# Turning the first chunk's residual by VectorE blocks and a trip through memory in place of four TensorE transposes

## The reference, cut to what matters

```
xn = layernorm(layernorm(x)) * ln_g + ln_b
q, k, v = split(xn @ W_qkv + b_qkv)
gate = sigmoid(layernorm(x) @ W_gate + b_gate); gate /= mean(gate) + 1e-5
q, k = relu(q * gate)**2 + 1e-5, relu(k * gate)**2 + 1e-5
# scan over time, per head: kv += k^T v; ks += k; out = (q @ kv) / (q . ks + 1e-5)
x1 = x + out @ W_proj + b_proj
P = layernorm(x1) @ U1                    # 512 -> 128
H = gelu(P @ V1 + b1)                     # 128 -> 2048
out = x1 + (H @ U2) @ V2 + b2             # 2048 -> 128 -> 512
```

## Time and profile before

| | |
|---|---|
| median of the runs | 1697.15 us |
| profiled execution | 1697.67 us, of which the span of the trace is 1695.9 us |
| PE busy | 1665.1 us (98%) |
| DVE busy | 1400.3 us (83%) |
| POOL, ACT busy | 900.2 us (53%), 630.5 us (37%) |
| x1t_lo, line 683 | 64 times, mean 681 ns |
| key blocks, line 737 | 64 times, mean 703 ns |

### The profile page before, as it was taken

One profiled execution on the slowest core, in us unless ns is written; L12 is line 12 of the kernel. 1 busy time (PEld: TensorE's weight loads), 2 busy tenths in 40 slices (PEclk: granted clock), 3 DMA queues, 4 the chain that ended last, 5 costly groups with the idle time before them and its releaser, 6 DMA issues.

```text
span 1695.9 us, 39553 instructions
## 1 busy us (share of the span) xinstructions
PE 1665.1 (98%) x16221; PEld 1401.9 (83%) x16221; DVE 1400.3 (83%) x2223; ACT 630.5 (37%) x1178; POOL 900.2 (53%) x1026
## 2 busy tenths in 40 slices
PE   6899999999999999999999999999999999999998
PEld 4688888888888888888888888888888888888876
DVE  6888888888888888888888888888888888888875
ACT  4233333333333333433433333333333333333332
POOL 3355555555555555555555555555555555555540
PEclk9999999999999999999999999999999999999999
DMA  8323323333322333342333233343223323322210
GB/s 231 88 58 70 59 75 46 72 75 57 72 72 45 74 70 60 73 71 47 74 72 59 73 62 56 74 69 61 74 49 69 75 57 70 74 45 73 58 45 26
DMA packets 206324, 115.67 MB, mean 68 GB/s; under 512 B 151144, under 2 KB 161792, under 8 KB 206144
## 3 DMA queue, kind: packets, MB, share of 16 engines
q1 hardware_dynamic: 205280, 111.57, 31.4%
q10 hardware_dynamic: 864, 1.57, 0.5%
HBM read 79.38 MB, written 33.72 MB: 67 GB/s over the span
## 4 chain that ended last, share of the span: by engine, by line
PE 93%; DVE 3%; DMA 1%; issue 1%; SPq 1%; ACT 0%; POOL 0%; DVEq 0%; POOLq 0%
PE ps_a L849 11%; PE ps_a L850 10%; PE ps_a L851 10%; PE scores L849 8%; PE scores L851 8%; PE scores L850 8%; PE ps_h L849 4%; PE ps_h L850 4%; PE ps_h L851 4%; PE scores L980 4%; PE scores L1008 4%; PE ps_q L849 3%; PE ps_q L850 3%; PE ps_q L851 3%; PE scores L856 3%; PE ps_a L1026 2%
## 5 line engine op out<-in xcount | busy, mean ns | idle before, releaser
L447 POOL TENSOR_TENSOR h_lo<-h_full,h_hi 128x512 fp32r<-128x512 f32 x244 | 336.4, 1389 | 220.4 <-DVE h_hi L665 219.0
L849 PE MATMUL ps_a<-wx_hi,zt_hi 128*128 128x512 f32 x768 | 315.7, 411 | 6.3 <-DVE key_sums L787 4.2
L850 PE MATMUL ps_a<-wx_lo,zt_hi 128*128 128x512 f32 x768 | 305.1, 397 | 0.0
L851 PE MATMUL ps_a<-wx_hi,zt_lo 128*128 128x512 f32 x768 | 305.0, 397 | 0.0
L530 ACT ACTIVATE h_full<-ps_h,cols 128x256 f32<-128x256 f32 x512 | 204.5, 476 | 144.1 <-PE ps_h L851 137.6
L849 PEld LDWEIGHTS ps_a<-wx_hi,zt_hi 128*128 128x128 f32 x768 | 145.3, 189 | 43.2 <-DVE zt_lo L620 7.1
L665 DVE CAST h_hi<-h_full 128x512 fp32r<-128x512 f32 x256 | 163.3, 648 | 17.8 <-ACT h_full L530 13.7
L851 PEld LDWEIGHTS ps_a<-wx_hi,zt_lo 128*128 128x128 f32 x768 | 145.1, 189 | 35.6
L850 PEld LDWEIGHTS ps_a<-wx_lo,zt_hi 128*128 128x128 f32 x768 | 145.3, 189 | 28.7 <-issue 0.5
L541 ACT ACTIVATE query_t<-scores 128x512 f32<-128x512 f32 x64 | 38.3, 599 | 345.9 <-PE scores L856 345.9
L467 POOL TENSOR_TENSOR key_lo<-keys,key_hi 128x512 fp32r<-128x512 f32 x64 | 86.9, 1358 | 121.1 <-ACT key_hi L561 121.1
(11 more groups left out here) (156 smaller groups left out, 4230.7 us busy)
## 6 DMA issues: line engine op xcount, KB each, us to landing
xs<-L_attn_x SPq DMA_DIRECT2D x64, 256.0 KB, 4.1
key_blocks<-zs SPq DMA_DIRECT2D x64, 256.0 KB, 2.0
key_t<-key_blocks SPq DMA_DIRECT2D x256, 64.0 KB
out<-x1s SPq DMA_DIRECT2D x64, 256.0 KB, 2.1
xt<-x_turned SPq DMA_DIRECT2D x63, 256.0 KB, 4.2
key_sums<-carry_rows SPq DMA_DIRECT2D x60, 256.0 KB, 3.7
rows<-turned_rows SPq DMA_DIRECT2D x63, 64.0 KB, 4.5
x1s<-L_attn_W_gate SPq DMA_DIRECT2D x4, 256.0 KB, 4.2
```

The costliest lines, as they stand in the source:

```text
L447: E.tensor_tensor(h_lo[:, i % SLOTS, :], h_full[:, i % SLOTS, :], h_hi[:, i % SLOTS, :].bitcast(F32), ALU.subtract).then_inc(s["h_lo_ready ...
L849: E.matmul(ps, wh, mh, start=start and i == 0, stop=False)
L850: E.matmul(ps, wh, ml, start=False, stop=False)
L851: mm = E.matmul(ps, wl, mh, start=False, stop=stop and i == last)
```

## The change

The first chunk of each pair (`half == 0`) isn't turned by PE any more. In the even step DVE turns `zs` in 32 x 32 blocks into the first quarter of `probs`, right behind the gate (`turn_residual`); SP writes that to a new DRAM tensor `residual_blocks` and reads it back into `zs` by four DMAs of 128-byte pieces. ACT makes `x1t_hi` from `zs` late in the same even step, and DVE makes `x1t_lo` from `zs` at the step's end, between the moments of x1 and the new `zs`. The key blocks go to `gate` instead of `zs`, and the second use of `gate` (line 794) waits until they have been written out. The second chunk of each pair is turned as before.

```diff
+    def pair(self, per=1):
+
+        return per * ((4 * self.p + self.off) // 2 + 1)
...
@@ -338,6 +343,14 @@
+                d = Chunk(p, b - 2)
+                if d.exists and d.half == 0:
+
+                    sp.wait_ge(s["res_out"], d.pair(16))
+                    for j in range(HPG):
+                        sp.dma_start(zs[j * HEAD:(j + 1) * HEAD, :].rearrange("d (f a t) -> d f a t", f=KT, t=HEAD),
+                                     res_dram.rearrange("(a d) (f j t) -> j d f a t", d=HEAD, f=KT, t=HEAD)[j])\
+                            .then_inc(res_in[j], 16)
...
-                    sp.dma_start(blocks_dram, zs[:, :]).then_inc(s["blocks_out"], 16)
+                    sp.dma_start(blocks_dram, gate[:, :]).then_inc(s["blocks_out"], 16)
...
+                before = Chunk(p, b - 1)
+                if before.exists and before.half == 0:
+
+                    sp.wait_ge(s["res_ready"], before.pair())
+                    for j in range(HPG):
+                        wait(sp, res_in[j], before.pair(16) - 16)
+                    sp.dma_start(res_dram, probs[:, 0, :]).then_inc(s["res_out"], 16)
                 load_x(Chunk(p, b + 3))
...
@@ -546,8 +566,8 @@
-                if d.exists:
-                    act.wait_ge(s["tx_done"], d.done())
+                if d.exists and d.half:
+                    act.wait_ge(s["tx_done"], d.pair())
                     E.activation(x1t_hi[:, :, d.half * P:(d.half + 1) * P],
                                  ps_t[:, :].rearrange("p (k n) -> p k n", k=KT), ACT.Copy)\
                         .then_inc(s["x1t_hi_ready"], 1)
...
                     gelu(ffn, pairs[2])
                     gelu(ffn, pairs[3])
+                if d.exists and d.half == 0:
+                    for j in range(HPG):
+                        act.wait_ge(res_in[j], d.pair(16))
+                    E.activation(x1t_hi[:, :, 0:P], zs[:, :].rearrange("p (k n) -> p k n", k=KT), ACT.Copy)\
+                        .then_inc(s["x1t_hi_ready"], 1)
+                if ffn.exists:
...
+                def x1t_from_bank():
+                    if d.half:
+                        x1t_tail(ps_t)
+
+                def turn_residual():
+
+                    if d.exists and d.half == 0:
+                        dve.wait_ge(s["z1_ready"], d.done())
+                        E.transpose(probs[:, 0, :], zs[:, :]).then_inc(s["res_ready"], 1)
...
                         .then_inc(s["gate_evac"], 1)
+                    turn_residual()
 
                     dve.wait_ge(s["gate_sig"], n.done())
...
-                    if d.exists:
-                        dve.wait_ge(s["tx_done"], d.done())
-                    elif c.exists:
-                        dve.wait_ge(s["blocks_out"], c.done(16, 16))
-                    else:
-                        dve.wait_ge(s["tz_done"], 1)
-                    E.transpose(zs[:, :], keys[:, n.half, :]).then_inc(s["blocks_ready"], 1)
+                    E.transpose(gate[:, :], keys[:, n.half, :]).then_inc(s["blocks_ready"], 1)
                 if c.exists:
                     dve.wait_ge(s["scores_done"], c.done())
                     blocks = HPG * KT
+                    if d.exists and d.half == 0:
+                        dve.wait_ge(s["res_out"], d.pair(16))
...
                     dve.wait_ge(s["query_steps"], n.done(3, 3))
+                    dve.wait_ge(s["blocks_out"], n.done(16, 16))
...
                     E.bn_aggr(moments1[:, :], stats1[:, :]).then_inc(s["x1_steps"], 1)
+                if d.half == 0:
+                    x1t_tail(zs)
+                if c.exists:
                     dve.wait_ge(s["x1_small"], c.done(2, 2))
-                    if d.exists:
-                        dve.wait_ge(s["tx_done"], d.done())
+                    if d.exists and d.half == 0:
+                        dve.wait_ge(s["x1t_ready"], d.done())
+                    if d.exists and d.half:
+                        dve.wait_ge(s["tx_done"], d.pair())
                     elif not c.p and not c.off:
                         dve.wait_ge(s["tz_done"], 1)
-                    if n.exists:
-                        dve.wait_ge(s["blocks_out"], n.done(16, 16))
...
```

More of the change, by code:

```diff
@@ L108, in block_kernel @@
 def block_kernel(nc, x, ln_g, ln_b, w_qkv, b_qkv, w_gate, b_gate, w_proj, b_proj,
-                 u1, v1, b1, u2, v2, b2, x_turned, out, carry_dram, rows_dram, blocks_dram):
+                 u1, v1, b1, u2, v2, b2, x_turned, out, carry_dram, rows_dram, blocks_dram, res_dram):
     ctx = ExitStack()
@@ L207, in block_kernel @@
             query_done query_steps value_done value_ready
-            sums_done den_steps blocks_ready blocks_out tq_done query_t_ready
+            sums_done den_steps blocks_ready blocks_out res_ready res_out tq_done query_t_ready
             scores_done probs_ready state_done state_ready ot_done ot_hi_ready ot_ready
@@ L215, in block_kernel @@
         xt_in = [sem(f"xt_in{i}") for i in range(4)]
+        res_in = [sem(f"res_in{j}") for j in range(HPG)]
         key_t_in = [sem(f"key_t_in{j}") for j in range(HPG)]
@@ L677, in step, with x1t_tail @@
                 finishing = is_last(p)
-                def x1t_tail():
+                def x1t_tail(turned):
                     if d.exists:
@@ L682, in x1t_tail @@
                         part = slice(d.half * P, (d.half + 1) * P)
-                        E.tensor_tensor(x1t_lo[:, :, part], ps_t[:, :].rearrange("p (k n) -> p k n", k=KT),
+                        E.tensor_tensor(x1t_lo[:, :, part], turned[:, :].rearrange("p (k n) -> p k n", k=KT),
                                         x1t_hi[:, :, part].bitcast(F32), ALU.subtract).then_inc(s["x1t_ready"], 1)
+                def x1t_from_bank():
[5 more added lines that the diff above has]
+                        E.transpose(probs[:, 0, :], zs[:, :]).then_inc(s["res_ready"], 1)
                 if n.exists:
@@ L704, in step @@
                     squared_relu(n, s["key_done"], s["key_steps"], ps_b, KEY, keys[:, n.half, :],
-                                 x1t_tail)
+                                 x1t_from_bank)
                 else:
-                    x1t_tail()
+                    turn_residual()
+                    x1t_from_bank()
                 if b % 2:
@@ L1070 @@
     blocks_dram = nc.dram_tensor("key_blocks", (P, DM), _mybir.dt.float32, kind="Internal").ap()
+    res_dram = nc.dram_tensor("residual_blocks", (P, DM), _mybir.dt.float32, kind="Internal").ap()
     rows_dram = nc.dram_tensor("turned_rows", (BATCHES, P), _mybir.dt.float32, kind="Internal").ap()
-    block_kernel(nc, *args, out, carry_dram, rows_dram, blocks_dram)
+    block_kernel(nc, *args, out, carry_dram, rows_dram, blocks_dram, res_dram)
     r = _run(nc, [arrays], core_ids=[0])
```

## The result

The changed kernel takes 1688.12 us (median of four runs, 1685.22 to 1688.72) against 1697.08 for the kernel before: ratio 0.9945 (95% interval 0.9928 to 0.9962), 9.0 us gained. Five more rounds on another chip gave 1687.6 against 1695.92, ratio 0.9959 (0.9946 to 0.9972). I had predicted 1682.3 with a range of 1680.3 to 1687. The direction was right, the size wrong by 5.8 us.

The account below looks back on a forecast made before the run. PE was taken to bound the kernel, busy 98% of the span. Gains of 13.2 (steady part), 0.1 (start) and 1.6 (drain) sum to 14.9 us, giving 1682.3 us, range 1680.3 to 1687.

Parts of the forecast that it names:

- What PE loses: PE's stream, each pair: the first chunk's four transposes go, 0.44 us a pair, 13.2 us for 30 pairs.
- The block transpose on DVE: Even step, behind the gate: 0.70 us more on DVE fits into its 1.69 us idle wait for ACT's sigmoid; costs nothing.
- The mask's new wait: DVE's mask in the even step: the residual's write lands in 2.0 us, leaving 4.7 us of slack.
- SP's queue: SP in the even step: x loads start 1.5 us later harmlessly; four reads issued by 838.3, slack 2.1 us.
- the landing of the reads: Reload of `zs` for ACT: lands about 4.8 us after the first issue, over 7 us of slack.
- rival 3: Mask's wait on `res_out`: the trip through memory lands late, at 842.0; 35 us lost against 15 gained, about 1717; 5%.
- The low part in the moments' gap: Even step's end: `x1t_lo` beside POOL's two operations delays the new `zs` by 0.3 us, hidden in the steady part.
- Start: First even step: `x1t_lo` leaves DVE's chain (0.38 us), the gap grows 0.3; gain 0.1, bounds +0.4 and -1.0.
- Drain: Last even step: mask waits for the residual's write, gain 1.9 us, less 0.3 for the gap; net 1.6, bounds 1.9 and 0.
- Rivals 1 and 2: 1: moments' gap too small, 1691.9, 10%. 2: DVE is the real bound, only the drain's gain stays, 1695.6, 5%.

Follow-up runs that it names:

- the drain's edit: Changed kernel with chunk 0's key blocks in `zs`; in the last even step the residual's blocks also go to `gate`, so the mask waits for no write: 1681.84 us.
- the spare products: 8 unused products while PE idles before the mask's first use in the last even step, added to chunk 0's write on ACT's queue and residual in `gate`: 1677.18 us.
- the kernel with three spare writes: Changed kernel with chunk 0's key blocks in `zs`; three extra writes of the turned residual, each landed before the real one is issued: 1841.31 us in one run.

## Why the prediction was wrong, step by step

- *What PE loses*: right. 13.2 predicted for 30 pairs, 14.2 measured (0.47 a pair for 0.44; the 1 us is more than the 0.02 a pair that I allowed for the reading). Other traces with the same steady part have 50.90 a pair, 13.0 in 30.
- *The block transpose on DVE*: right; 0.70 us, and the wait for the sigmoid fell from 1.69 to 1.05 (1.0 predicted).
- *The mask's new wait, SP's queue, the landing of the reads*: right in the steady part. The write's landing had a median of 2.7 us and not 2.0, at most 4.5, all inside the slack. The bound of 4.8 for the reads was misread, as 20 slices of 0.45 us from 1634 end at 1643.0 and not 1643.5; they landed in 2.3 to 4.8 all the same, with a slack of 7. One more write in front changed nothing, three took the slack away: rival 3 is a real mechanism, at a landing that doesn't happen.
- *The low part in the moments' gap*: right in size, 0.35 later against the 0.3 taken, but for a reason that I had argued against. I took POOL to run on beside the subtraction. It is held up until that has ended; the rule that two SBUF inputs of VectorE contend with GpSimd (the Trainium skill, GPSIMD Engine Reference, 1. Specifications) is what the runs show, with 0.19 against 0.55 us. The subtraction itself took 0.66 and not its upper bound of 1.45.
- *Start*: wrong, and the cause of the miss. Predicted +0.1 with bounds of +0.4 and -1.0; measured -5.0. I counted what was removed from DVE's chain (the 0.38 of `x1t_lo`) and what was added to the gap, and left out the wait that the diff adds ahead of the second use of `gate`. The clue was in my own rows: a landing of 8.4 us, which I priced only as a rival for the residual's write. It was the key blocks' first write. In the kernel before, the added wait alone costs 6.5 us by the medians, and with the write issued 6 us sooner, on ACT's queue, line 829 waits for nothing and the changed kernel takes 1682.59.
- *Drain*: predicted 1.6, measured 0.8. The mask came 1.9 sooner, as said, and the gap took 0.36, as said. Not in the sum was that PE's longer idle time keeps the clock at the half level longer, 0.7 us.
- Rivals 1 and 2 were wrong: no new wait of PE with 30 entries, and DVE had the room.

The sum by what was measured: 14.2 - 5.0 + 0.8 = 10.0 in the traces (9.0 by the medians), and the range, 1680.3 to 1687, was wrong for the same reason as the sum: it held bounds for every edit but that one.

## What to carry to other kernels

Count every wait that a diff adds, and price each by the worst landing of its DMA and not by the median: a maximum of 8.4 beside a median of 2.0 is one particular transfer, so find where it stands. A buffer that is reused sooner turns a landing that nobody waited for into one on the chain, first of all in the start, where the kernel before has 8.4 and 4.6 us for its first two writes. When a landing is late, look at what was issued behind it on its queue as well as at what stood ahead. Where TensorE has to idle for a few microseconds at either end, the wait can cost its own length and a half-speed stretch behind it; the write on another queue, the drain's edit and the spare products together took the kernel from 1687.6 to 1677.18.

## What the runs showed of the hardware

- A write of 256 KB whose median landing is 2.0 us took 6.5 to 11.5 us in 24 cases, in each with a write of 512 bytes in 4-byte pieces issued 0.5 to 2.8 us behind it on SP's queue. Loads just ahead weren't needed (four of the 24, in the steady part of the kernel with three spare writes, 9.5 to 10.8 us) and didn't do it alone: four second writes, issued 0.2 us behind the last weight load but with the small write 3.4 us or more behind them, landed in 4.4 to 4.6. Nor is the small write enough: 34 others had it 1.0 to 2.9 us behind them, before they had landed, and landed in 2.2 to 3.2. No experiment separates these causes.
- The late landing isn't busy DMA engines: in the changed kernel the DMA share is 0.00 in the window of 45 to 48 us, and the landing comes at 47.55. What holds it until then the traces don't show.
- PE's clock fell to its half level behind idle times of 2.03, 2.37 and 4.66 us, and behind one of 2.37 it did not (last pair 12.60 us). With PE kept busy by spare products, so that about 0.3 us of idle time was left, it didn't fall in any of three traces.
- A 128x1 operation of POOL takes 0.55 and not 0.19 us when it starts beside a DVE subtraction of 128x512 with two SBUF inputs, and ends 0.05 us after it, in 48 steps of 48; with one input in PSUM it keeps its 0.19.
